# A graph network on one core: wider spread operations, row products spread over the sort, hats made earlier, a gather ring of 4 slots of 8 tiles

## The chip, the core and the metric

The kernel runs on one core of a Trainium2 chip. The metric is the device time of one execution in microseconds (us). The core has five engines with queues of their own: TensorE (PE in the profile; its weight loads PEld), VectorE (DVE), ScalarE (ACT), GpSimd (POOL) and SyncE (SP). They meet through semaphores only. Each engine works its own queue in order, so an instruction that waits holds all that is behind it.

## The reference

There are 12,500 nodes with 32 features and 200,000 edges (`src`, `dst`, and three edge attributes). Edges come sorted by `dst`. Two layers are added to `x`.

```python
def spline_conv(x, row, col, basis, idx, W, b):      # W: [125, Fin, Fout]
    z = jnp.einsum('ni,kio->nko', x, W).reshape(N * K, Fout)
    msg = jnp.einsum('es,eso->eo', basis, z[col[:, None] * K + idx])
    out = segment_sum(msg, row, N)
    return out / jnp.maximum(deg, 1.0)[:, None] + b

# layer 0: h = relu(layernorm(x)), row = src, col = dst
h1 = elu(spline_conv(ones, ..., stn1_w, stn1_b))      # 1 -> 64
h2 = elu(spline_conv(h1, ..., stn2_w, stn2_b))        # 64 -> 64
t = elu(h2 @ stn3_w + stn3_b) @ stn4_w + stn4_b       # a shift of 3 words per node
new_pseudo = clip(pseudo + t[col] - t[row], 0, 1)
x = x + spline_conv(h, ..., basis(new_pseudo), conv_w, conv_b)   # 32 -> 32

# layer 1: h = relu(layernorm(x)); graph attention with 4 heads, then a GRU gate
alpha = softmax over the edges of a dst of leaky_relu(el[src] + er[dst], 0.2)
agg = segment_sum(feat[src] * alpha, dst)
x = x + elu(gru(agg, h))
```

The basis of an edge is the product of three one-dimensional degree-1 "hats" over five knots each, so 125 numbers of which eight are not zero.

## The kernel before

All edges are padded to 1568 tiles of 128. The program is a row of phases, each a block of five engine programs with a barrier behind it.

**Sort** (`sort_edges`). Edges are put in the order of `src` by counting. A step of the loop is a group of G = 8 tiles; there are 196 groups, and two buffers `u` take turns. VectorE makes one-hot matrices of a tile's low and high key digits (`hots`, L462 and L464). TensorE transposes the low ones (L519), adds each pair of tiles to a running table in PSUM (`run`, L541), and looks the keys of each tile up in the table so far (`look`, L546). ScalarE copies the table out between two steps (L578). For the rank inside a tile, TensorE lays the tile's keys out along rows, one float32 product a tile (`rows`, L525), and VectorE compares and counts (L486). VectorE multiplies the look by the high one-hot (L491) and adds both into `place` (L496). GpSimd then scatters the eight tiles' records to memory (L600). TensorE's loop over a group has four steps `k`; each adds two tiles, looks two tiles up, and after step 1 the function `turn` issues the transposes and the row products of the next group, all together.

**First convolution** (`conv_of_ones`). 98 blocks of 128 nodes, each with 18 tiles of edges, with two buffers. SyncE loads the records of a block (L704), once TensorE has ended the block two before. ScalarE copies words into `keep` and computes parts of the hats (`hat_sides`), VectorE the rest of the hats (L744), the plane of two hats (L747), the one-hot of nodes (`mark`, L725) and the basis (L730). TensorE sums 18 products into `acc` (L782), ScalarE takes the sums (L821), and every second block TensorE mixes them with the weights. ScalarE also stores `keep` to memory (L818). In ScalarE's program a block is: hats, store, take the sums; every second block also two results.

**Second and third convolution** (`flow_conv`, called twice). GpSimd gathers node rows for all edges, a tile at a time (L913), and stores them (L920). SyncE waits until the tiles that a block needs have been stored, then loads the windows of a block: 32 windows of four nodes, 128 edges each, in two halves `q` of 16 (L974), and for the third convolution a row of shifts for each half (`trow`, L978). VectorE multiplies the mark of an edge's node by its features (`make_spread`, L1032), two windows at a time, into `spread`, eight pieces a half; in the third convolution these pieces stand between the steps of the new hats. TensorE multiplies basis and spread of each window into one of four PSUM banks (L1158); a bank holds one piece, and ScalarE empties it into `sums` (L1244). With `feats` = 64 a piece fills 512 columns of a bank, with 32 it fills 256. SyncE loads the next half when all spreads of the half before it have been made.

**Attention** (`attention_flow`). GpSimd gathers rows of `gat_table` into a ring of AT_RING = 8 slots of AT_SLOT = 4 tiles (L1528); SyncE stores each full slot (L1497) and loads the next indices for it (L1475). After a turn of 32 tiles GpSimd loads the runs of edges of two blocks of nodes (L1543), once all slots are stored and VectorE has made the products of the pair before. VectorE computes softmax weights and products (L1687), TensorE sums 41 products a block (L1774), ScalarE takes them (L1733), and VectorE and ScalarE compute the gate.

## Time and profile before

| | |
|---|---|
| three runs, median (lowest, highest) | 15029.32 us (15001.8, 15085.03) |
| the profiled execution | 14974.48 us |
| its span | 14972.8 us |
| mean granted TensorE clock | 0.721 |
| busy: TensorE, VectorE, ScalarE, GpSimd | 56%, 46%, 20%, 49% |

The profile is of one execution. A line such as L525 is a line of the kernel. "Idle before" is the time an engine was idle ahead of a group of instructions, with what ended the wait; "issue" stands for waits that ended with nothing that the profile shows, "remote" for one where the semaphore was raised well after the modelled end of all that could have raised it. The granted clock is a share of 2.4 GHz; it is 0.50 or 1.00 at any moment. A float32 product has two records.

### The profile page before, as it was taken

Reading aid. Unit: us, or ns where it says so; the run is one execution under the profiler, and the core shown is the slowest. Engines: PE = TensorE matmul, PEld = TensorE weight load, DVE = VectorE, ACT = ScalarE, POOL = GpSimd, SP = SyncE. Lnnn points to the kernel's source line nnn. Section 1 sums busy time; section 2 is a strip of 40 time slices with the busy share of each in tenths; the row PEclk is TensorE's granted clock in tenths of the full one; section 3 lists DMA queues with packets and bytes.
Section 4 is the critical chain, followed back from the end, with each engine's and each line's share of the span. In section 5 each row is a group of like instructions: output and inputs, shape, how many; then the busy total and the mean of one; then the engine's idle time right before and its main releaser. Section 6 shows DMA issues by size and latency. Waiting matters only on the chain. (4 is left out here: it accounts for less than half of the span.)

```text
span 14972.8 us, 221170 instructions
## 1 busy us (share of the span) xinstructions
PE 8457.1 (56%) x56706; PEld 7263.5 (49%) x56706; DVE 6837.4 (46%) x17239; ACT 2974.3 (20%) x9191; POOL 7273.4 (49%) x7456
## 2 busy tenths in 40 slices
PE   3466666653553777777897555555552444444445
PEld 2455555553553656665786444444552333333334
DVE  9644444443444444444676444444672222232223
ACT  0011111111111223232343222222340000000001
POOL 4355555550000888888301778878103444444442
PEclk9866666666776888888998666666885666666666
DMA  1200000006111444444332333333221111111111
GB/s 34 79 2 2 2 2 2 2 2 17 19 19 35 81 76 79 77 79 77 67 57 50 50 48 50 51 48 52 45 42 23 38 41 37 37 36 40 37 37 38
DMA packets 1831366, 603.46 MB, mean 40 GB/s; under 512 B 1616773, under 2 KB 1772389, under 8 KB 1831074
## 3 DMA queue, kind: packets, MB, share of 16 engines
q1 hardware_dynamic: 1119378, 307.87, 11.1%
q0 software_dynamic: 255648, 274.30, 10.1%
q10 hardware_dynamic: 456304, 20.89, 2.6%
q8 instruction: 13, 0.21, 0.0%
q14 instruction: 23, 0.19, 0.0%
HBM read 429.15 MB, written 172.95 MB: 40 GB/s over the span
## 5 line engine op out<-in xcount | busy, mean ns | idle before, releaser
L1158 PE MATMUL c_acc<-c_spread_sb,c_basis_sb 128*125 128x256 f32 (+1 forms) x12544 | 2750.6, 383 | 967.1 <-issue 420.5
L1158 PEld LDWEIGHTS c_acc<-c_spread_sb,c_basis_sb 128*125 128x125 f32 x12544 | 2294.3, 231 | 1335.4 <-issue 699.8
L1774 PE MATMUL at_acc_ps<-at_prod,ident 128*128 128x128 f32 x8036 | 1294.3, 312 | 1913.1 <-issue 1521.4
L600 POOL DMA_INDIRECT rec<-rk_rec,rk_place x1568 | 1620.0, 1033 | 1211.7 <-DVE rk_place L496 776.7
L1774 PEld LDWEIGHTS at_acc_ps<-at_prod,ident 128*128 128x128 f32 x8036 | 1185.7, 225 | 2022.0 <-issue 2021.6
L1528 POOL DMA_INDIRECT at_ring<-gat_table,at_place x1568 | 1486.1, 948 | 1362.2 <-issue 1311.3
L913 POOL DMA_INDIRECT c_ring<-hid_table,c_at x1568 | 1639.5, 1046 | 478.9 <-issue 463.3
L913 POOL DMA_INDIRECT c_ring<-feat_table,c_at x1568 | 1587.6, 1013 | 478.1 <-issue 463.8
L1032 DVE TENSOR_TENSOR c_spread_sb<-c_mark,c_rin 128x512 f32<-128x512 f32 (+1 forms) x3136 | 1746.0, 557 | 53.8
L1244 ACT ACTIVATE c_sums<-c_acc 125x512 f32<-125x512 f32 (+1 forms) x3136 | 1441.1, 489 | 1363.7 <-PE c_acc L1158 1062.7
L1172 PE MATMUL c_mix<-c_sums,c_w 125*64 125x128 f32 (+1 forms) x18816 | 1275.2, 300 | 525.5 <-issue 409.6
L1172 PEld LDWEIGHTS c_mix<-c_sums,c_w 125*64 125x64 f32 (+1 forms) x18816 | 992.1, 138 | 808.7 <-issue 648.9
L546 PE MATMUL rk_look_ps<-rk_table,rk_lo_t 128*128 128x98 f32 x3136 | 878.7, 412 | 713.2 <-DVE rk_before L491 682.0
L908 POOL COPY c_at<-dst_at 128x16 uint32 (+1 forms) x196 | 60.4, 308 | 2335.8 <-POOLq L1854 2335.0
L546 PEld LDWEIGHTS rk_look_ps<-rk_table,rk_lo_t 128*128 128x128 f32 x3136 | 668.5, 278 | 834.5 <-DVE rk_before L491 777.3
L491 DVE CUSTOM_DVE_ANT_0 rk_junk_l<-rk_look_ps,rk_hi 128x98 bf16<-128x98 f32 x1568 | 403.7, 257 | 1424.8 <-remote 1246.7
L782 PE MATMUL c_acc<-c_mark,c_basis_sb 128*125 128x128 f32 x3528 | 643.3, 367 | 714.5 <-DVE c_basis_sb L730 714.5
L1612 DVE COPY gr_hs<-h 128x64 f32 (+1 forms) x49 | 9.6, 195 | 2251.4 <-ACT acc L1733 2251.4
L782 PEld LDWEIGHTS c_acc<-c_mark,c_basis_sb 128*125 128x125 f32 x3528 | 627.5, 279 | 727.7 <-issue 727.7
L1543 POOL DMA_INDIRECT at_run<-rows,at_run_at x98 | 93.8, 958 | 1402.3 <-issue 1402.3
L578 ACT ACTIVATE rk_table<-rk_run_ps 128x98 f32<-128x98 f32 x784 | 198.3, 253 | 2327.1 <-remote 1204.9
L525 PE MATMUL rk_rows_ps<-ident,rk_cols 128*128 128x128 f32 x3152 | 654.6, 393 | 0.0
(358 smaller groups left out, 10906.2 us busy)
## 6 DMA issues: line engine op xcount, KB each, us to landing
c_rin<-rows SPq DMA_DIRECT2D x3136, 42.0 KB
c_rin<-rows SPq DMA_DIRECT2D x3136, 20.0 KB
rows<-c_ring POOLq DMA_DIRECT2D x392, 128.0 KB
rows<-rk_blank SPq DMA_DIRECT2D x112, 252.0 KB
rows<-c_ring POOLq DMA_DIRECT2D x392, 72.0 KB
rows<-at_ring SPq DMA_DIRECT2D x392, 72.0 KB
rec<-rk_rec,rk_place POOLq DMA_INDIRECT x1568
c_ring<-hid_table,c_at POOLq DMA_INDIRECT x1568
```

Of the source, the lines that this page charges most:

```text
L491: dve.tensor_tensor_reduce(junk_l[:, u, j, :], look[:, j % 2, 0:NB], hi_hot[:, u, j, :], 1.0, 0.0, ALU.mult, ALU.add, before[:, u, j:j + 1 ...
L525: last = pe.matmul(rows[:, u, j, :], bc(cols[:, u, j:j + 1], [P, P]), c.ident[:, :], start=True, stop=True)
L546: pe.matmul(look[:, j % 2, 0:NB], lo_t[:, u, j, :], table[:, k % 2, :], start=True, stop=True).then_inc(looked, 1)
L600: pool.indirect_dma_start(out=d.rec, out_offset=bass.IndirectOffsetOnAxis(ap=place[:, u, j:j + 1], axis=0), in_=rec[:, u, j, :], in_offset ...
L782: last = pe.matmul(acc[u][:, 0:P], basis[:, u, t, :, :].rearrange("p a b -> p (a b)"), mark[:, u, t, :], start=(t == 0), stop=(t == BT - 1))
L913: pool.indirect_dma_start(out=ring[:, u, j, :], out_offset=None, in_=table, in_offset=bass.IndirectOffsetOnAxis(ap=at[:, h, u, j:j + 1], a ...
L1032: dve.tensor_tensor(spread[:, q, w, :, :], bc(mark[:, q, w, :].unsqueeze(2), [P, 2, feats, WN]), bc(rin[:, q, w, 0:feats].unsqueeze(3), [P ...
L1158: last = pe.matmul(acc[pp % BANKS][:, (w % 2) * WN * feats:(w % 2 + 1) * WN * feats], basis[:, q, w, :, :].rearrange("p a b -> p (a b)"), ...
L1172: last = pe.matmul(mix[k * outs:(k + 1) * outs, 0:P], wsb[:, f, :], sums[:, f, :], start=(i == 0), stop=(i == each - 1))
L1244: act.activation(sums[:, :, pp * 2 * WN:(pp + 1) * 2 * WN].rearrange("p f (k n) -> p k f n", n=WN), acc[pp % BANKS][:, 0:pair].rearrange(" ...
L1528: pool.indirect_dma_start(out=ring[:, u, j, :], out_offset=None, in_=d.gat_table, in_offset=bass.IndirectOffsetOnAxis(ap=place[:, u, j:j + ...
L1774: last = pe.matmul(acc_ps[:, v, 0:P], c.ident[:, :], prod[:, v, s, :, :].rearrange("p h f -> p (h f)"), start=(s == 0), stop=(s == RUN))
```

## The change

Four parts.

1. Third convolution: a spread operation covers four windows (`span` = 4), a bank holds four windows (512 columns), a half has four pieces in place of eight, and the eviction takes 512 columns. Spread 0 follows the selection, spread 1 the subtraction of positions, spread 2 the clipping, spread 3 the plane. The second convolution keeps two windows.
2. Sort: the row products of the next group are no longer in `turn` but in `rows_of`, two of the eight after each of the four steps.
3. First convolution: ScalarE prepares (copies, hats) blocks 0 and 1 ahead of its loop. In the loop, for each block it stores, takes the sums, and prepares the block two on; then it takes the two results. `bend` has two buffers.
4. Attention: 4 slots of 8 tiles, and GpSimd no longer waits for the gathers of two slots before. A turn still has 32 tiles.

```diff
-AT_RING = 8
-AT_SLOT = 4
+AT_RING = 4
+AT_SLOT = 8
...
-                pe.wait_ge(cols_made, g + 1)
-                for j in range(G):
+            def rows_of(g, u, k):
+                if k == 0:
+                    pe.wait_ge(cols_made, g + 1)
+                for j in (2 * k, 2 * k + 1):
                     last = pe.matmul(rows[:, u, j, :], bc(cols[:, u, j:j + 1], [P, P]), c.ident[:, :],
                                      start=True, stop=True)
-                last.then_inc(rows_made, 1)
+                if k == G // 2 - 1:
+                    last.then_inc(rows_made, 1)
...
                         if k == 1:
                             turn(g + 1, 1 - u)
+                        rows_of(g + 1, 1 - u, k)
...
-            def body(b, pair, u):
+            def prepare(b, pair, u):
                 item = pair * 2 + u
                 act.wait_ge(loaded[u], pair * 16 + 16)
                 act.wait_ge(kept, item * 16 + 16)
...
+            def store(b, pair, u):
+                item = pair * 2 + u
                 act.wait_ge(copied, item * 2 + 6)
                 act.wait_ge(hats_made, item * 2 + 2)
                 act.wait_ge(kept, item * 16 + 32)
+                act.sem_inc(act_turn, 1)
...
+            with act.Fori(0, n) as o:
+                offsets.next_pass(act, o)
+                for u in range(2):
+                    prepare(u, o * (NB // 2), u)
+                with act.Fori(0, NB // 2 - 1) as h:
+                    pair = o * (NB // 2) + h
+                    for u in range(2):
+                        store(h * 2 + u, pair, u)
+                        take_sums(pair * 2 + u, u)
+                        prepare(h * 2 + u + 2, pair + 1, u)
+                    for u in range(2):
+                        take(h * 2 + u, pair * 2 + u, u)
...
-    pieces = GW2 // 2
+    span = 2 if moved is None else 4
+    pieces = GW2 // span
...
-    pair = 2 * WN * feats
+    pair = span * WN * feats
...
-                        w = slice(k * 2, k * 2 + 2)
+                        w = slice(k * span, k * span + span)
...
                 .then_inc(seq, 1)
-                make_spread(1)
                 after_step(5)
                 dve.tensor_tensor(pos[:, q, :, :], pos[:, q, :, :], tsrc[:, :, :], ALU.subtract).then_inc(seq, 1)
-                make_spread(2)
+                make_spread(1)
                 after_step(6)
...
-                make_spread(3, 4, 5)
+                make_spread(2)
...
-                make_spread(6)
                 after_step(8)
                 make_plane(hat[:, q, :, :, :])
-                make_spread(7)
+                make_spread(3)
...
-                    if u >= 2:
-                        pool.wait_ge(gathered[u - 2], t * (16 * AT_SLOT) + 16 * AT_SLOT)
-                        pool.sem_inc(pool_turn, 1)
```

## Rows read from the trace of the kernel before

**Rows 1.** Busy time by stage: sort, first convolution, third, attention.
```profile
522.00:3357.00 2835.00, 1723.37 (x9434) 1552.50 (x9434) 1320.68 (x6868) 462.50 (x1966) 1621.20 (x1570) 0.65 0.05 13
3357.00:4765.00 1408.00, 684.62 (x3921) 671.33 (x3921) 623.24 (x788) 240.81 (x980) 0.00 (x0) 0.74 0.28 19
...
8161.00:11265.00 3104.00, 1678.64 (x12916) 1387.34 (x12920) 1527.57 (x3728) 877.66 (x2938) 1920.60 (x2058) 0.69 0.32 48
...
11410.00:14973.00 3563.00, 1486.08 (x8629) 1308.81 (x8629) 1039.59 (x2426) 257.26 (x540) 1579.93 (x1666) 0.62 0.17 37
```
**Rows 2.** Waits in the sort: total us, times, longest.
```profile
DVE rk_junk_l L491 <- remote: 1246.7, 190, 8.1
...
POOL rec L600 <- DVE rk_place L496: 776.7, 196, 14.2
```
**Rows 3.** Timeline of TensorE in one group of the sort.
```profile
2025.21 1.33 PE L546 MATMUL rk_look_ps<-rk_table,rk_lo_t 128*128 128x98 f32 x4 [2.26 <-DVE rk_before L491]
...
2027.19 3.73 PE L525 MATMUL rk_rows_ps<-ident,rk_cols 128*128 128x128 f32 x16
...
2030.88 0.84 PE L546 MATMUL rk_look_ps<-rk_table,rk_lo_t 128*128 128x98 f32 x4
```
**Rows 4.** Timeline of VectorE in the same group.
```profile
2022.60 1.23 DVE L462 TENSOR_TENSOR rk_lo<-ramp_bf,src_lo 128x1024 bf16<-128x1024 bf16 x1 [0.50 <-issue]
2023.74 0.97 DVE L464 TENSOR_TENSOR rk_hi<-ramp_bf,src_hi 128x784 bf16<-128x784 bf16 x1
...
2033.59 0.26 DVE L491 CUSTOM_DVE_ANT_0 rk_junk_l<-rk_look_ps,rk_hi 128x98 bf16<-128x98 f32 x1 [6.46 <-remote]
```
**Rows 5.** The line L821 in the first convolution, and what it waited for.
```profile
L821 ACT ACTIVATE c_sums<-c_acc x98: 277/278/278, 3480.3 to 4763.1; 125x128 f32<-125x128 f32 x98
...
  PE c_acc L782: 1006.3, 97
```
**Rows 6.** Timeline of one block of the first convolution.
```profile
3903.47 0.28 ACT L821 ACTIVATE c_sums<-c_acc 125x128 f32<-125x128 f32 x1 [10.36 <-PE c_acc L782]
...
3904.40 13.51 SPq L704 DMA_DIRECT2D c_rin<-rec  x2
...
3905.71 0.41 DVE L744 SCALAR_TENSOR_TENSOR c_keep<-c_keep,c_sides 128x54 f32<-128x54 f32 x2 [6.20 <-ACT c_keep L654]
...
3909.44 7.09 PE L782 MATMUL c_acc<-c_mark,c_basis_sb 128*125 128x128 f32 x36 [6.00 <-DVE c_basis_sb L730]
```
**Rows 7.** Two microseconds of that block: busy times, then the granted clock.
```profile
3907.00:3908.00 1.00, 0.00 (x0) 0.00 (x0) 1.00 (x2) 0.00 (x0) 0.00 (x0) 1.00 0.00 0
...
3910.00:3911.00 1.00, 1.00 (x6) 1.00 (x6) 0.97 (x3) 0.00 (x0) 0.00 (x0) 0.50 0.00 0
```
**Rows 8.** Groups of the third convolution by form.
```profile
L1032 DVE TENSOR_TENSOR c_spread_sb<-c_mark,c_rin 128x256 f32<-128x256 f32 x1568 | 660.5, 421 | 13.5
```
**Rows 9.** The same operation in the second convolution.
```profile
L1032 DVE TENSOR_TENSOR c_spread_sb<-c_mark,c_rin 128x512 f32<-128x512 f32 x1568 | 1085.4, 692 | 40.3
```
**Rows 10.** Third convolution: SyncE in the gathers; SyncE and VectorE behind them.
```profile
9217.00 11.14 SPq L974 DMA_DIRECT2D c_rin<-rows  x16
...
10821.44 0.33 SPq L978 DMA_DIRECT2D c_trow<-move  x1
10822.67 8.99 SPq L974 DMA_DIRECT2D c_rin<-rows  x16
...
10824.86 0.23 DVE L1060 TENSOR_SCALAR c_rel<-c_rin,first 128x16 f32<-128x16 f32 x1 [2.65 <-DMA c_trow<-move]
```
**Rows 11.** The row loads of the third convolution, to 10560 and from there.
```profile
L978 SPq DMA_DIRECT2D c_trow<-move x133: 3/333/718, 8209.0 to 10557.2; - x133
...
L978 SPq DMA_DIRECT2D c_trow<-move x63: 332/333/333, 10569.0 to 11248.1; - x63
```
**Rows 12.** Attention: GpSimd's timeline at a run load, and waits of the stage.
```profile
12334.99 0.97 POOL L1543 DMA_INDIRECT at_run<-rows,at_run_at  x1 [29.34 <-issue]
...
PE at_acc_ps L1774 <- issue: 1521.4, 902, 3.2
```

More of the change, by code:

```diff
@@ L520, in turn @@
                 last.then_inc(turned, 1)
-                pe.wait_ge(cols_made, g + 1)
-                for j in range(G):
+            def rows_of(g, u, k):
+                if k == 0:
+                    pe.wait_ge(cols_made, g + 1)
+                for j in (2 * k, 2 * k + 1):
                     last = pe.matmul(rows[:, u, j, :], bc(cols[:, u, j:j + 1], [P, P]), c.ident[:, :],
                                      start=True, stop=True)
-                last.then_inc(rows_made, 1)
+                if k == G // 2 - 1:
+                    last.then_inc(rows_made, 1)
             pe.matmul(run[:, 0:NB], c.ident[:, :], c.base[:, 0, :], start=True, stop=True).then_inc(updated, 1)
             turn(0, 0)
+            for k in range(G // 2):
+                rows_of(0, 0, k)
             with pe.Fori(0, NG // 2) as i:
@@ L672, in conv_of_ones @@
     sides_made, bent, hats_made = sem("c1_sides"), sem("c1_bent"), sem("c1_hats")
+    act_turn = sem("c1_act_turn")
     steps = 3
@@ L678, in conv_of_ones @@
         rel = sb("c1_rel", [P, BT])
-        sides, bend = sb("c1_sides", [P, 2, BT, 3, 2]), sb("c1_bend", [P, BT, 3])
+        sides, bend = sb("c1_sides", [P, 2, BT, 3, 2]), sb("c1_bend", [P, 2, BT, 3])
         keep = sb("c1_keep", [P, 2, BT, KEEP])
@@ L819, in body, with take_sums @@
                               keep[:, u, :, :]).then_inc(kept, 16)
+            def take_sums(item, u):
                 act.wait_ge(summed, item + 3)
                 act.activation(sums[:, u, :], acc[u][:, 0:P], ACT.Copy).then_inc(sums_taken, 1)
-                if u == 1:
-                    take(b - 1, item - 1, 0)
-                    take(b, item, 1)
-            block_loop(act, c.block_passes[:, 0:1], body, before=lambda o: offsets.next_pass(act, o))
+            n = act.value_load(c.block_passes[:, 0:1], min_val=1, max_val=EP // BROWS + 1)
+            with act.Fori(0, n) as o:
[10 more added lines that the diff above has]
+                        take(h * 2 + u, pair * 2 + u, u)
+                pair = o * (NB // 2) + NB // 2 - 1
+                for u in range(2):
+                    store(NB - 2 + u, pair, u)
+                    take_sums(pair * 2 + u, u)
+                for u in range(2):
+                    take(NB - 2 + u, pair * 2 + u, u)
             act.wait_ge(indexed, 16)
@@ L1030, in make_spread @@
                     for k in ks:
-                        w = slice(k * 2, k * 2 + 2)
-                        dve.tensor_tensor(spread[:, q, w, :, :], bc(mark[:, q, w, :].unsqueeze(2), [P, 2, feats, WN]),
-                                          bc(rin[:, q, w, 0:feats].unsqueeze(3), [P, 2, feats, WN]), ALU.mult)\
+                        w = slice(k * span, k * span + span)
+                        dve.tensor_tensor(spread[:, q, w, :, :], bc(mark[:, q, w, :].unsqueeze(2), [P, span, feats, WN]),
+                                          bc(rin[:, q, w, 0:feats].unsqueeze(3), [P, span, feats, WN]), ALU.mult)\
                             .then_inc(spread_made, 1)
@@ L1244, in take_sums @@
                         act.activation(
-                            sums[:, :, pp * 2 * WN:(pp + 1) * 2 * WN].rearrange("p f (k n) -> p k f n", n=WN),
-                            acc[pp % BANKS][:, 0:pair].rearrange("p (k f n) -> p k f n", k=2, n=WN), ACT.Copy)\
+                            sums[:, :, pp * span * WN:(pp + 1) * span * WN].rearrange("p f (k n) -> p k f n", n=WN),
+                            acc[pp % BANKS][:, 0:pair].rearrange("p (k f n) -> p k f n", k=span, n=WN), ACT.Copy)\
                             .then_inc(taken, 1)
```

14 lines of the change are left out of this document (7 added, 7 removed).

## The prediction

> **What bounds the kernel now.** I read the page's 40 slices first, then the busy time by stage, then in each stage the waits and one period of the timeline. The program is five stages with barriers between them, on one core, so the gains add up. No engine is full in any stage [rows 1]: in each one a loop of waits sets the pace.
>
> The sort handles 196 groups in 2835 us, 14.46 us each [rows 1]. VectorE is busy 6.7 us of that (1320.68/196). Its largest wait, 1246.7 us in 190 waits, 6.56 us each, is for the look product of tile 4 [rows 2]. In the timeline TensorE runs the transposes and then all 16 row-product records in one block of 3.73 us before that look; VectorE, idle 6.46 us, resumes at 2033.59, though the last look record was begun by 2030.88 and lasts 0.84 us by the model [rows 3, 4]. So 1.9 us of the wait is TensorE being later than its modelled ends. GpSimd issues eight scatters and then waits 776.7/196 = 3.96 us for the places [rows 2, 4]; without that wait a group takes 14.46 - 3.96 = 10.5 us, the floor of the stage.
>
> The first convolution runs 98 blocks. After the first they come every 13.23 us ((4763.1 - 3480.3)/97), and ScalarE waits 1006.3/97 = 10.4 us of that for TensorE [rows 5]. The timeline is a ring with nothing beside it: ScalarE takes the sums at 3903.47, only then makes the hats, VectorE, idle 6.20 us for them, goes on at 3905.71, TensorE starts at 3909.44 after 6.00 us idle and works 7.09 us [rows 6]. ScalarE makes the next hats behind the sums in its own queue, though the records had long landed.
>
> The third convolution takes 3104 us [rows 1]. While GpSimd gathers (to 10560) SyncE issues 133 half-block loads, one in (10557.2 - 8209.0)/132 = 17.8 us; afterwards one in (11248.1 - 10569.0)/62 = 10.95 us [rows 11]. In the second part SyncE is full: sixteen loads are 8.99 us, the rest is offsets and the row load [rows 10]. So that tail is SyncE's, not VectorE's or ScalarE's.
>
> Attention takes 3563 us [rows 1]. GpSimd is idle 29.34 us before its run load in each period and 1402.3 us in all [rows 12]; TensorE waits 1521.4 us for nothing that the profile shows [rows 12].
>
> **The change, part by part.**
>
> *Sort.* The same 16 row records are issued, two products (4 records) after each pair of looks. No instruction and no DMA is added. From the stretch before look 4, 12 records go: 12 x 3.73/16 = 2.8 us [rows 3]. The four records of step 0 fall in TensorE's 2.26 us wait for VectorE [rows 3], those of step 3 behind the last look, under VectorE's two one-hot operations (1.23 and 0.97 us, 2.2 us [rows 4]); the four of step 2 stand before look 6, where VectorE now hardly waits: up to 0.93 us comes back. That is 1.9 us a group. The 1.9 us by which TensorE lags after the block may go too, which makes 3.8. Bounds: 1.0 us (a second of the spread pairs is paid in full) and 3.96 us (GpSimd's floor, [rows 2]). I take 2.9, midway of 1.9 and 3.8, since the lag follows the block each time: 196 x 2.9 = 568 us, range 196 to 776. If VectorE's operations no longer cover the last pair, it costs 0.93 us a group, 182 us.
>
> The lag is TensorE waiting for nothing the profile names. The Trainium skill, page "Runtime: NRT & Kernel Launch", section "Instruction fetch mechanics", says that instructions are fetched ahead and that this hides except at branches; by it the lag would not be hunger for instructions and could stay, and the sum would be 196 us poorer. The trace bears it out only in part: attention's unnamed TensorE gaps lie inside a straight run of products [rows 12].
>
> *First convolution.* ScalarE now makes the hats for block i+2 right after the sums of block i, ahead of block i+1's, so VectorE builds a basis while TensorE multiplies. Its store waits for the same hats and now stands before the sums; the final two takes of a pair stand last. Nothing is added but a second bend tile and one semaphore step. Three loops remain. VectorE: 623.24 us less the 6 us of clearing, over 98, is 6.3 us a block [rows 1]. TensorE: 7.09 us plus some 0.4 us of mixing, 7.5, at 1.2 GHz; at 2.4 GHz about half. The load ring spans two blocks: sums to load issue 0.93 us, about 3.1 us to its landing (an estimate from the third convolution, where VectorE goes on 3.1 us after the end of the row load's issue [rows 10]), hats 2.05 (the 2.24 us from 3903.47 to 3905.71, less some 0.2 for the sums' own copy), VectorE up to the first basis half 3.7, product 7.1 [rows 6]: 16.0/2 = 8.0 us; with the product at 2.4 GHz 6.2. The granted clock is 0.50 at 3910 and 1.00 at 3907, during and after the last third of a block [rows 7]: TensorE earns 2.4 GHz late in each block and loses it in the idle 6 us that now go. So I take 7.5 us, between 6.6 (VectorE with its gaps) and 8.4: 97 x (13.23 - 7.5) = 556 us, range 97 x 4.8 = 468 to 97 x 6.6 = 640. The first 120 us, to 3480.3 [rows 1, 5], stay. If a loop I do not see adds 1 us, 97 us are lost; 360 us is my lower end.
>
> The Trainium skill, page "TensorE: Matmul & The Clock Gate", Part 1, has the slow clock as the default that sustained work lifts. [rows 7] agree; by that rule alone this stage would run at 2.4 GHz throughout and VectorE would set about 6.7 us, 78 us better than the sum.
>
> *Third convolution.* VectorE's 1568 spreads of 421 ns become 784 of about 692 ns, as the second convolution's operation of 512 columns [rows 8, 9]: 660 to 543 us of busy time and half of the waits. ScalarE's evictions shrink likewise. A TensorE bank holds four windows, so it can run 16 windows ahead of ScalarE, not 8. None of this touches SyncE's tail: 63 halves stay at 10.95 us. In the gather phase a half costs 17.8 us where SyncE alone needs about 14.3 (11.14 for sixteen loads [rows 10], the rest as in the tail, with its longer gaps); 3.5 x 133 = 465 us is waiting for the others. If a quarter of it goes (my choice between none and all, nearer to none, since VectorE's spreads are two fifths of its busy time there [rows 1, 8] and half of them go), 116 us are eight more halves during the gathers, hence some 85 to 100 us off the tail. I take 100; ends 0 (the loads' own order holds) and 300 (all waiting gone). A loss would need spread 3 to hold back the basis: 0.69 us against 0.42, which is hidden under SyncE's 11 us.
>
> *Attention.* The gathers (1568), their order and the turns of 32 tiles stay. Stores go from 392 of 72 KB to 196 of 144 KB, place loads halve, and GpSimd loses six waits a turn, each of which cost under 0.3 us. The last store of a turn is twice as large and starts after eight gathers; that is covered by the 29 us of [rows 12]. SyncE issues half as many DMAs while TensorE is starved. I take 1 us of 45 periods, 40 us; ends -30 and 150.
>
> Sum: 568 + 556 + 100 + 40 = 1264 us. The profiled execution took 14974.48 us (span 14972.8), so 13,710 us; it stands 0.36% under the median 15029.32 of three runs, so in their terms 13,760.
>
> **Rivals.**
>
> *A. Forecast:* all four as above, 13,760; its own range 13,500 to 14,000. Chance 0.55.
>
> *B. The sort falls to GpSimd's floor* and the first convolution to VectorE's: 776 + 640 + 150 + 40 = 1606, so 13,420. For it: the lag comes with the block, and the average load of TensorE in the sort is only 61%. Against: ScalarE copies the records only after the scatters of two groups ago have landed, which leaves no slack at 10.5 us. Chance 0.15.
>
> *C. The spread products are not hidden:* each pair is followed by its own lag, and the sort gives 1.0 us a group, the rest as in A: 196 instead of 568, so 14,130. For it: the lag appears only while GpSimd issues scatters, and GpSimd would now issue nearly all the time. Against: 2.26 us of TensorE's wait lies in such a stretch. Chance 0.24.
>
> *D. Slower:* the last pair of row products, now behind look 7 in TensorE's queue, becomes what VectorE waits for at each group's start. It costs nothing up to 2.2 us after look 7, and one for one beyond. To cancel the other gains (696 us) a group must take 14.46 + 3.55 = 18.0 us, so the pair must come 3.55 us plus all of the saved 2.8 us late, over 8 us after look 7; with 10 us it would be 15,100. Nothing in the rows is that late but gaps under starvation. Chance 0.03.
>
> *E. The convolution's order does nothing:* ScalarE still stands behind something, say the store's landing, and its stage gains under 2 us a block: about 14,100. Chance 0.03.
>
> The range that leaves out no more than 2 in 10 reaches from B to past C: 13,350 to 14,250. A measurement here tells a change from none at about 0.5%. Faster by more 0.96, within 0.01, slower 0.03.
>
> **What would show it.** The sort: VectorE's wait for the look under 3.5 us and GpSimd's wait for places near 1 us, a stage of about 2270 us. First convolution: a block in 7.5 us, TensorE idle under 1 us, clock near 1.0 for most of it, a stage of about 850 us. Third: fewer than 63 halves after the last gather, the tail still 10.95 us each. Attention: period still near 71 us. The prediction is wrong if the sort's wait only moves to other looks, if a block takes over 9 us, or if attention's period shifts by more than 3 us, which nothing in my rows lets me foresee.

## The result and the profile after

The changed kernel takes 14,424.83 us (median of 4 runs, 14,398.6 to 14,469.58) where the kernel before takes 15,015.56 us (median of 4): ratio 0.9606, interval 0.9558 to 0.9654. That is 591 us or 3.9 per cent off, well under the 1,264 us forecast and outside the range, on its slow side.

The first view is the same table of stages, after: sort, first, second and third convolution, attention. It has busy times in the order TensorE, weight loads, VectorE, ScalarE, GpSimd, then the granted clock, the DMA share and GB/s.

```profile
522.00:3246.00 2724.00, 1753.68 (x9434) 1556.07 (x9434) 1320.55 (x6868) 464.39 (x1966) 1616.46 (x1570) 0.65 0.05 13
3246.00:4179.00 933.00, 573.56 (x3921) 553.34 (x3921) 627.49 (x788) 234.37 (x980) 0.00 (x0) 0.79 0.43 28
4230.00:7650.00 3420.00, 2702.65 (x19894) 2187.10 (x19894) 1758.67 (x2849) 1110.93 (x2744) 1963.66 (x2059) 0.87 0.35 71
7650.00:10792.00 3142.00, 1619.28 (x12920) 1342.48 (x12924) 1439.72 (x2944) 772.03 (x2154) 1892.32 (x2057) 0.67 0.29 47
10937.00:14468.00 3531.00, 1485.69 (x8629) 1304.14 (x8629) 1039.70 (x2426) 254.96 (x539) 1577.82 (x1666) 0.62 0.15 38
```

Against [rows 1]: the sort gains 111 us (568 forecast), the first convolution 475 (556), attention 32 (40). The third convolution is 38 us longer where I had 100 off, and the second, whose code is unchanged, 75 longer (3420 against 3345). Sum: 505 us, as the two profiled executions differ (14,974.48 and 14,469.58). The medians differ by 591, because the first profiled execution lay 41 us under its median and the second 45 over; so 86 us of these stage differences belong to the pair of executions and not to the change.

The sort's largest waits after the change, in the manner of [rows 2]:

```profile
ACT rk_table L584 <- PE rk_run_ps L546: 1224.3, 387, 5.3
ACT rk_table L584 <- remote: 920.3, 196, 7.6
DVE rk_junk_l L491 <- remote: 811.7, 192, 7.9
POOL rec L606 <- DVE rk_place L496: 614.6, 180, 4.5
...
DVE rk_junk_l L491 <- PE rk_look_ps L551: 492.5, 304, 2.8
```

Before, the row beside the first of [rows 2] was

```profile
DVE rk_junk_l L491 <- PE rk_look_ps L546: 119.6, 133, 6.4
```

So VectorE's two largest waits for looks have gone from 1246.7 + 119.6 = 1366 us to 811.7 + 492.5 = 1304, in more and shorter pieces, and GpSimd's wait before its first scatter from 776.7 to 670 us (614.6, and 55.7 in 16 groups for ScalarE's records), 4.0 to 3.4 us a group. One group of the timeline says where the long piece lies now: the last steps of TensorE, then ScalarE, VectorE and GpSimd, each with the idle time before it in brackets.

```profile
2009.83 1.17 PE L527 MATMUL rk_rows_ps<-ident,rk_cols 128*128 128x128 f32 x4
...
2012.79 0.37 PE L546 MATMUL rk_run_ps<-rk_hi,rk_lo 128*128 128x98 bf16 x2
2012.96 1.42 PE L551 MATMUL rk_look_ps<-rk_table,rk_lo_t 128*128 128x98 f32 x4
2014.17 1.11 PE L527 MATMUL rk_rows_ps<-ident,rk_cols 128*128 128x128 f32 x4
2017.29 0.32 PE L546 MATMUL rk_run_ps<-rk_hi,rk_lo 128*128 128x98 bf16 x2 [2.00 <-ACT rk_table L584]
```
```profile
2016.89 0.25 ACT L584 ACTIVATE rk_table<-rk_run_ps 128x98 f32<-128x98 f32 x1 [4.89 <-remote]
```
```profile
2011.89 0.26 DVE L491 CUSTOM_DVE_ANT_0 rk_junk_l<-rk_look_ps,rk_hi 128x98 bf16<-128x98 f32 x1 [2.13 <-PE rk_look_ps L551]
...
2017.62 0.26 DVE L491 CUSTOM_DVE_ANT_0 rk_junk_l<-rk_look_ps,rk_hi 128x98 bf16<-128x98 f32 x1 [3.77 <-remote]
```
```profile
2006.04 1.26 POOL L606 DMA_INDIRECT rec<-rk_rec,rk_place  x1 [3.52 <-DVE rk_place L496]
...
2015.24 0.97 POOL L606 DMA_INDIRECT rec<-rk_rec,rk_place  x1 [0.30 <-issue]
```

Read the ScalarE line against the second of TensorE's. The copy at 2016.89 waits for the run products recorded at 2012.79, 0.37 us long by the model: 4.1 us pass before ScalarE may go on, and they end 0.7 us after the eighth scatter does (2015.24 + 0.97 = 2016.21). VectorE's wait before look 4 has shrunk from 6.46 to 2.13 us as forecast, and before look 6, where I had written "VectorE now hardly waits", 3.77 us have appeared. The eighth scatter of the group before the change, which [rows 4] do not show, was

```profile
2032.64 0.97 POOL L600 DMA_INDIRECT rec<-rk_rec,rk_place  x1 [0.31 <-issue]
```

It ends at 2033.61, and VectorE's long wait had ended at 2033.59. So the wait ended with GpSimd's burst before the change as well, and the group shown is no exception: in 171 groups of the sort (between 600 and 3300 us) the wait before look 4 ended 0.0 us (median) from the end of the burst, and after the change, in 171 of 175 groups, that before look 6 ends 1.4 us behind it. The spread products let two more looks through during the burst; the last two still come when it is over.

The first convolution: ScalarE's sums, what it waits for, and its timeline over one block.

```profile
L834 ACT ACTIVATE c_sums<-c_acc x98: 277/277/278, 3369.3 to 4174.0; 125x128 f32<-125x128 f32 x98
```
```profile
ACT c_keep L816 <- DMA rows<-c_keep: 198.3, 49, 4.3
ACT c_keep L816 <- DMA c_rin<-rec: 187.6, 47, 4.7
```
```profile
3909.76 0.57 ACTq L829 DMA_DIRECT2D rows<-c_keep  x1
3910.45 0.28 ACT L834 ACTIVATE c_sums<-c_acc 125x128 f32<-125x128 f32 x1 [1.38 <-DVE c_keep L751]
3914.66 0.24 ACT L816 ACTIVATE c_keep<-c_rin 128x18 f32<-128x18 f32 x1 [3.94 <-DMA rows<-c_keep]
...
3916.33 0.39 ACT L660 ACTIVATE c_keep<-c_bend,knots 128x54 f32<-128x54 f32 x1
...
3917.94 0.57 ACTq L829 DMA_DIRECT2D rows<-c_keep  x1
```

A block takes (4174.0 - 3369.3)/97 = 8.30 us instead of 13.22. And a wait is here that [rows 6] did not have: ScalarE stores the records of a block and then, next in its order, wants to write the next but one into the same buffer, so it waits 3.94 us for its own store to land. From one store to the next it is 8.18 us. That is every second block (49 waits); in the others the load of the records lands last (47 waits), which is the load ring of the prediction.

### The profile page after: what moved, and what is told of

It is laid out like the page before. It is cut to its first block and busy times, and to the rows that moved or that the text cites. A ratio compares the mean times of both kernels' runs of the same rounds, so it can differ in the third digit from the quotient of the medians.

```text
span 14467.9 us, 214500 instructions
## 1 busy us (share of the span) xinstructions
PE 8371.9 (58%) x56706; PEld 7125.0 (49%) x56706; DVE 6752.7 (47%) x16455; ACT 2861.0 (20%) x8407; POOL 7219.1 (50%) x7456
## 3 DMA queue, kind: packets, MB, share of 16 engines
q1 hardware_dynamic: 1062354, 307.85, 10.5%
## 5 line engine op out<-in xcount | busy, mean ns | idle before, releaser
L1186 PE MATMUL c_acc<-c_spread_sb,c_basis_sb 128*125 128x256 f32 (+1 forms) x12544 | 2557.0, 368 | 464.7 <-issue 227.4
L1186 PEld LDWEIGHTS c_acc<-c_spread_sb,c_basis_sb 128*125 128x125 f32 x12544 | 2170.7, 220 | 768.6 <-issue 487.5
L606 POOL DMA_INDIRECT rec<-rk_rec,rk_place x1568 | 1615.3, 1030 | 1105.1 <-DVE rk_place L496 614.6
L1200 PE MATMUL c_mix<-c_sums,c_w 125*64 125x128 f32 (+1 forms) x18816 | 1454.3, 329 | 1136.6 <-issue 610.6
L1200 PEld LDWEIGHTS c_mix<-c_sums,c_w 125*64 125x64 f32 (+1 forms) x18816 | 1085.2, 150 | 1491.0 <-issue 914.4
L1062 DVE TENSOR_TENSOR c_spread_sb<-c_mark,c_rin 128x512 f32<-128x512 f32 x2352 | 1622.8, 690 | 40.3
L1272 ACT ACTIVATE c_sums<-c_acc 125x512 f32<-125x512 f32 x2352 | 1328.8, 596 | 1255.5 <-PE c_acc L1186 852.5
L491 DVE CUSTOM_DVE_ANT_0 rk_junk_l<-rk_look_ps,rk_hi 128x98 bf16<-128x98 f32 x1568 | 402.9, 257 | 1314.0 <-remote 811.7
L527 PE MATMUL rk_rows_ps<-ident,rk_cols 128*128 128x128 f32 x3152 | 768.8, 389 | 2.6 <-ACT rk_cols L561 2.1
L527 PEld LDWEIGHTS rk_rows_ps<-ident,rk_cols 128*128 128x128 f32 x3152 | 663.0, 291 | 5.2 <-ACT rk_cols L561 5.2
L486 DVE SCALAR_TENSOR_TENSOR rk_junk<-rk_rows_ps,src_f,rk_earlier 128x128 bf16<-128x128 f32 (+1 forms) x1568 | 647.9, 413 | 2.8 <-PE rk_rows_ps L527 2.8
L950 POOL DMA_DIRECT2D rows<-c_ring x784 | 626.9, 800 | 11.6 <-DMA c_ring<-hid_table,c_at 6.8
```

The costliest lines, as they stand in the source:

```text
L486: dve.scalar_tensor_tensor(junk[:, u, j // 2, odd:2 * odd + 1, :], rows[:, u, j - odd:j + 1, :], c.src[:, bass.ds(g * G + j, 1)], earlier[ ...
L527: last = pe.matmul(rows[:, u, j, :], bc(cols[:, u, j:j + 1], [P, P]), c.ident[:, :], start=True, stop=True)
L606: pool.indirect_dma_start(out=d.rec, out_offset=bass.IndirectOffsetOnAxis(ap=place[:, u, j:j + 1], axis=0), in_=rec[:, u, j, :], in_offset ...
L950: pool.dma_start(rows_v[:, bass.ds(t * tiles + u * slot, slot), :], ring[:, u, :, :]).then_inc(stored[u], 16)
L1062: dve.tensor_tensor(spread[:, q, w, :, :], bc(mark[:, q, w, :].unsqueeze(2), [P, span, feats, WN]), bc(rin[:, q, w, 0:feats].unsqueeze(3), ...
L1186: last = pe.matmul(acc[pp % BANKS][:, (w % span) * WN * feats:(w % span + 1) * WN * feats], basis[:, q, w, :, :].rearrange("p a b -> p (a ...
```

## The experiments

**Four parts, each alone on the kernel before.** The edits are the hunks of the diff: sort; first convolution; third convolution; attention's ring.

> The kernel before with the spread row products of the sort alone. If the parts act each in their own stage, the sort takes about 2724 us instead of 2835, every other stage is as before (second convolution near 3340, first 1408, third 3104, attention 3563) and the run stands 111 us below the kernel before. If the stage's loss against my 568 us came from another part of the change, this run gains 400 us or more. If the second convolution is near 3415 here too, its loss of 75 us comes with the sort's part.

> The kernel before with the new order of ScalarE in the first convolution alone. Parts act in their own stage: first convolution 933 us instead of 1408, the run 475 us below the kernel before. Rival, the gain is given back later: the second convolution takes 3415 us instead of 3340 and the run gains only 400 us.

> The kernel before with four windows per spread operation and per bank in the third convolution alone. Parts act in their own stage: third convolution 3142 us instead of 3104, so the run is 38 us above the kernel before (0.25 per cent). Rival, the 38 us are chance between two executions: third convolution within 3090 to 3120 and no difference in the run. My prediction's term would be 100 us off (3004).

> The kernel before with attention's ring of 4 slots of 8 alone. Parts act in their own stage: attention 3531 us instead of 3563, the run 30 us below. Rival: the ring is nothing and the 30 us are chance; the run is within 10 us of the kernel before. If the second convolution is at 3415 here, its loss hangs on nothing in this change, since this part does not touch it.

These ran on a chip on which the kernel before takes 14,374 us (25 runs; it was not profiled there). Ratios and intervals: sort 0.9976 (0.9956 to 0.9996), hats 0.9729 (0.9713 to 0.9745), third convolution 0.9960 (0.9934 to 0.9986), ring 0.9992 (0.9967 to 1.0017). In their profiles a group of the sort takes 13.81 us with the spread and 14.01 to 14.04 in the three without; a half block of the third convolution 13.62 us with four windows and 13.85 to 14.14 in the others; a block of the first 8.46 and 13.22. The second convolution, from its first gather to that of the third, is 3102 to 3193 us in all four; none has it near the 3415 us of the rivals, though the same code varies by 91 us. So the hats are some four fifths of the gain of the parts, the four windows gain and do not lose, and the sort's part gains even less than the 111 us seen first. Two of the numbers are not what was expected. The hats' run stands 411 us under the kernel before and not 475, although its blocks give 97 x (13.22 - 8.46) = 462; the profiled execution, in which the second convolution is the shortest of the four, lies 101 us under its own median, so it does not show where the rest goes. And the ring is not told from nothing by the time of the run, but from its first gather on the attention stage takes 3472 us there and 3493 to 3502 in the other three.

**Sort stages with and without scatters, in one execution.** Three copies of the stage ahead of the real one; the copies write the same records to the same places, or none (with no scatters, GpSimd only raises the semaphore).

```diff
+            phase(lambda *a: sort_edges(*a, own=True, rows_at="block", scatter=False))
+            phase(lambda *a: sort_edges(*a, own=True, rows_at="spread", scatter=False))
+            phase(lambda *a: sort_edges(*a, own=True, rows_at="block"))
             phase(sort_edges)
```

> The changed kernel with three more sort stages ahead of the real one, which write the same records to the same places or none: (1) row products in one block, no scatters, (2) row products spread, no scatters, (3) block, with scatters, (4) spread, with scatters, the real one. Only the time of a group in each stage is read. Theory 1, TensorE's lag comes while GpSimd issues scatters, wherever the row products stand: with scatters about 14.0 (block) and 13.8 us (spread), as in the runs so far; without scatters 10.5 or less for the block and 1.9 to 2.8 us less for the spread. Rival 1, the chain between ScalarE's table copies and TensorE's runs sets the pace by its own latencies: without scatters still 13 us for both. Rival 2, my own working (the block is the delay and its lag comes with it): spread saves 2.9 us with scatters and without.

This chip ran the kernel before in 11,764 us. The starts of VectorE's place operation, 196 in each stage:

```profile
L500 DVE TENSOR_TENSOR rk_place<-rk_in_tile,rk_before x196: 166/168/170, 537.9 to 2534.7; 128x8 uint32<-128x8 f32 x196
L500 DVE TENSOR_TENSOR rk_place<-rk_in_tile,rk_before x196: 166/168/169, 2550.2 to 4154.9; 128x8 uint32<-128x8 f32 x196
L500 DVE TENSOR_TENSOR rk_place<-rk_in_tile,rk_before x196: 166/168/236, 4172.3 to 6268.5; 128x8 uint32<-128x8 f32 x196
L500 DVE TENSOR_TENSOR rk_place<-rk_in_tile,rk_before x196: 166/168/239, 6297.9 to 8431.0; 128x8 uint32<-128x8 f32 x196
```

Divided by 195 intervals: 10.24 (block) and 8.23 us (spread) without scatters, 10.75 and 10.94 with them. Without scatters the spread saves 2.0 us a group, my first sum of 1.9. With them, on this chip, it saves nothing, since eight scatters at 1.27 us are 10.2 us and GpSimd is nearly full. Rival 1, ScalarE's and TensorE's own latencies, falls: 8.23 is far under 13. Rival 2, my working, falls too.

**More products, other places.** Small products are four of one column at each step, into a row bank that is overwritten later.

```diff
+                        for _ in range(small):
+                            pe.matmul(rows[:, 1 - u, G - 1, 0:1], c.ident_bf[:, :], c.ident_bf[:, 0:1],
+                                      start=True, stop=True)
```

> The changed kernel with four more sort stages ahead: (1) spread with 16 more products of one column in each group (four at each step), no scatters, (2) the same with scatters, (3) all row products in steps 0 and 1, with scatters, (4) row products two pairs at step 0, one at step 1, one at step 2, none at step 3, with scatters, (5) the real stage. Theory 1, TensorE is short of instructions while GpSimd issues: the small products add 1.5 us or more a group with scatters and under 1 us without. Rival, they cost their time on the engine alone: the same addition in both. Placement: by theory 1 each is within 0.5 us of the real stage's 13.8; by the rival that the pair at step 3 is what VectorE waits for at the end of a group, (4) is 1 us or more faster.

Same chip: 8.49 us with 16 more products and no scatters (0.26 more), and with scatters 10.72 (small), 10.73 (all in steps 0 and 1), 10.98 (none at step 3), 10.96 (real). On this chip GpSimd hides everything, so the run does not tell theory and rival apart; it shows that 16 products cost 0.26 us where nothing covers them.

**The third convolution four times in one execution.**

```diff
+            phase(lambda *a: flow_conv(*a, "c3", ..., own=True, span=2))
+            phase(lambda *a: flow_conv(*a, "c3", ..., own=True, span=4, gather=False))
+            phase(lambda *a: flow_conv(*a, "c3", ..., own=True, span=2, gather=False))
             phase(flow_conv, "c3", ...)
```

> The changed kernel with three more third convolutions ahead of the real one (they write the same rows again, or read them without gathering): (1) two windows per spread, with gathers, (2) four windows, no gathers, (3) two windows, no gathers, (4) four windows, with gathers, the real one. Theory 1, SyncE's loads set the pace where nothing is gathered and the wider operation only helps during the gathers: without gathers both take 196 x 10.95 = 2146 us and the head, with gathers (4) is 40 to 100 us shorter than (1). Rival, four windows hold up the basis or the mixing: (2) is longer than (3), and (4) is at least 38 us longer than (1), as between the first two traces.

Same chip; SyncE's row loads, 196 halves each, in the order of the diff:

```profile
L1016 SPq DMA_DIRECT2D c_trow<-move x196: 332/333/362, 6342.5 to 8799.8; - x196
L1016 SPq DMA_DIRECT2D c_trow<-move x196: 332/333/333, 8834.3 to 10973.4; - x196
L1016 SPq DMA_DIRECT2D c_trow<-move x196: 332/333/333, 11009.6 to 13147.6; - x196
L1016 SPq DMA_DIRECT2D c_trow<-move x196: 332/333/409, 13214.7 to 15582.1; - x196
```

A half takes 12.60 us with two windows and gathers, 10.97 and 10.96 without gathers (four windows, two windows), 12.14 with four and gathers. The floor of SyncE's loads, 10.95 us in [rows 11], holds whatever VectorE does, and under gathers four windows save 0.46 x 195 = 90 us.

**The changed kernel on that chip.**

> The changed kernel itself, beside the parts on one chip. If the parts add up, the ratio to the kernel before is 0.9976 x 0.9729 x 0.9960 x 0.9992 = 0.966 and its second convolution is as long as in the kernels with one part (3102 to 3193 us). Rival, the second convolution loses some 75 us in it when all parts are in: ratio 0.971.

11,285.38 us, ratio 0.9592 (0.9576 to 0.9608); 479 us off. The parts give about the same: first convolution 97 x (13.22 - 8.70) = 438 (13.22 from the other chips, the kernel before was not profiled here), third 90, sort -37 (195 x 0.19). The product of the four parts' ratios, 0.966, was expected and is missed. The first convolution is a larger share of this shorter kernel, but on the like chip below it is 0.9591 as well, and the changed kernel was not run on the chip of the parts; so that the ratios multiply is not shown. Nothing can be said here of the second convolution's 75 us, as the chip has 2602 us for it. What differs from the first profile is every stage with gathers or scatters: the sort is 564 us shorter, second and third convolution 817 and 691, attention 1147, and the blocks of the first convolution 39 us longer, which sums to the whole difference of 3181 us but for 1. A group of the sort takes 10.93 us instead of 13.82, attention's period (11,222.5 - 9038.0)/48 = 46 us instead of 69. The sort's waits say that GpSimd sets its pace here and that ScalarE waits for the records of two groups ago to land, as the prediction's Rival B had against itself:

```profile
ACT rk_rec L580 <- DMA rec<-rk_rec,rk_place: 861.6, 193, 6.5
...
POOL rec L606 <- DVE rk_place L496: 20.4, 63, 1.5
```

The waits of attention, first on the first chip, then here:

```profile
PE at_acc_ps L1799 <- issue: 1424.2, 858, 132.7
...
POOL at_run L1568 <- issue: 1394.7, 98, 55.6
```
```profile
PE at_acc_ps L1799 <- DVE at_prod L1712: 1067.6, 49, 133.7
...
POOL at_run L1568 <- issue: 85.3, 98, 29.6
```

On the first chip TensorE stops 858 times inside its products for nothing that the profile names; here that wait is not listed; TensorE waits once a period for its operand, and GpSimd goes on without its 29 us of idle time.

**The same on a chip like the first** (kernel before 14,945 us): six sort stages, the kernel before for its stages, the changed kernel, and one further edit.

> The changed kernel with five more sort stages ahead: (1) block, no scatters, (2) spread, no scatters, (3) block, with scatters, (4) all row products in steps 0 and 1, with scatters, (5) spread with 16 more one-column products a group, with scatters, (6) the real one. On a chip where the kernel before takes 11,760 us the stages without scatters took 10.24 and 8.23 us a group, and those with scatters 10.75, 10.73, 10.72 and 10.94. Theory 1, TensorE is short of instructions while GpSimd issues, more so on some chips: where the kernel before takes 14,300 to 15,000 us, (1) and (2) are again 10.2 and 8.2 (nothing is issued there), (3) and (6) are 14.0 and 13.8, and (5) adds 0.5 us or more. Rival 1, such a chip is slower as a whole (memory, clock): (1) and (2) are also 20 per cent longer. Rival 2, only the scatters' landing is slower there: then (5) adds nothing. On a chip of the first kind the run repeats those numbers.

```profile
L500 DVE TENSOR_TENSOR rk_place<-rk_in_tile,rk_before x196: 166/168/170, 537.5 to 2533.8; 128x8 uint32<-128x8 f32 x196
L500 DVE TENSOR_TENSOR rk_place<-rk_in_tile,rk_before x196: 166/168/169, 2549.3 to 4146.6; 128x8 uint32<-128x8 f32 x196
L500 DVE TENSOR_TENSOR rk_place<-rk_in_tile,rk_before x196: 166/168/169, 4164.0 to 6964.9; 128x8 uint32<-128x8 f32 x196
L500 DVE TENSOR_TENSOR rk_place<-rk_in_tile,rk_before x196: 166/168/169, 6994.6 to 9707.1; 128x8 uint32<-128x8 f32 x196
L500 DVE TENSOR_TENSOR rk_place<-rk_in_tile,rk_before x196: 166/168/170, 9737.3 to 12467.5; 128x8 uint32<-128x8 f32 x196
L500 DVE TENSOR_TENSOR rk_place<-rk_in_tile,rk_before x196: 166/168/169, 12496.3 to 15198.0; 128x8 uint32<-128x8 f32 x196
```

10.24 and 8.19 us without scatters, to a few hundredths what the other chip has. With scatters: block 14.36, steps 0 and 1 13.91, small products 14.00, spread 13.85. So the chip is not slower as a whole (rival 1 falls); it is the scatters that cost 5.7 us a group (13.85 - 8.19) where the other chip has 2.7. But 16 more products cost 0.15 us and not the 0.5 or more that a shortage of instructions would ask: that half of theory 1 falls. Rival 2, a slower landing of the scatters, foretold just that. But no wait for their landing is listed in the sixth stage, and in the sort of the first pair only 24 us before the change and none after, where the chip of 11,764 us has 861.6 us of it. And it hardly matters where the row products stand.

> The kernel before, for its stages on this chip. If the first convolution issues no gathers and so is untouched by the chip, it has 13.22 us a block again, while the sort has between 10.75 and 14.4 us a group depending on the chip, and the second and third convolutions between 2600 and 3345 us.

14,932.6 us: 14.36 us a group, 13.22 a block of the first convolution, which issues no gathers, second and third convolution 3318 and 3259 us. All of it is as expected.

> The changed kernel again, for its ratio and its stages on this chip. If the kernel before takes 11,760 us here, 0.959 again; if it takes more, 0.960 to 0.970.

14,320.76 us, ratio 0.9591 (0.9547 to 0.9636), just under the 0.960 to 0.970 expected, with an interval that reaches into it. Its second convolution is 3355 us, and in two other kernels on this chip with the same code for it 3306 and 3339; its third 3212, the same code elsewhere on the chip 3160 and 3253, the kernel before 3259. With the 91 us between the four kernels of the parts, such spreads of one code (49 to 93 us) reach the 75 and 38 us that I had to explain.

**One more edit in the first convolution**, ScalarE's order again:

```diff
-                        store(h * 2 + u, pair, u)
+                        prepare(h * 2 + u + 1, pair + u, 1 - u)
                         take_sums(pair * 2 + u, u)
-                        prepare(h * 2 + u + 2, pair + 1, u)
+                        store(h * 2 + u + 1, pair + u, 1 - u)
```

> The changed kernel with one more edit of ScalarE's order in the first convolution: it prepares block b+1, takes the sums of b, then stores block b+1, so that a store has a whole block to land before its buffer is written again. Theory: the changed kernel's 8.3 to 8.7 us a block are the loop store (0.57) - landing (4.3) - hats (2.05) - VectorE's part and the store's semaphore (1.2), 8.2 us; now VectorE (6.3) or the load ring sets 6.7 to 7.6 us, 97 blocks gain 70 to 190 us and ScalarE's wait for the landing of its store goes. Rival, the load ring is the bound already: a block stays above 8 us.

A block takes 7.70 us instead of 8.45 on the same chip. ScalarE's waits for DMAs, first of the changed kernel, then with this edit:

```profile
ACT c_keep L816 <- DMA c_rin<-rec: 199.9, 49, 5.1
ACT c_keep L816 <- DMA rows<-c_keep: 196.5, 47, 4.7
```
```profile
ACT c_keep L816 <- DMA c_rin<-rec: 163.6, 95, 2.9
```

The wait for the store's landing is gone and the load's is what is left: 73 us off the stage, just short of what I expected (7.6 us at most). The run takes 14,284.39 us (14,273.25 to 14,295.69) against 14,320.76 (14,305.51 to 14,363.65), ratio to the kernel before 0.9563 (0.9521 to 0.9604). It is the fastest version on this chip, by 0.25 per cent; the intervals of the two ratios overlap, the runs do not. Of the stage's 73 us the medians keep 36.

**What about the scatters delays TensorE.** Spread row products in all stages; in place of the scatters GpSimd does nothing, copies, issues plain stores of the same records, or SyncE issues them.

```diff
+            phase(lambda *a: sort_edges(*a, own=True, scatter=False))
+            phase(lambda *a: sort_edges(*a, own=True, scatter=False, instead="copies"))
+            phase(lambda *a: sort_edges(*a, own=True, scatter=False, instead="plain"))
+            phase(lambda *a: sort_edges(*a, own=True, scatter=False, instead="sync"))
             phase(sort_edges)
```

> The changed kernel with four more sort stages ahead (spread row products in all): (1) no scatters, nothing in their place; (2) in their place eight copies of 512 words on GpSimd; (3) eight plain stores of the same records issued by GpSimd to one scratch place; (4) the same eight stores issued by SyncE; (5) the real stage with scatters. On a chip where (5) takes about 13.8 us against 8.2 for (1): if issuing DMAs from GpSimd delays TensorE, (3) is also 11 us or more while (2) and (4) stay under 9; if it is any activity of GpSimd, (2) is above 11 too; if it is the small packets of the records on the DMA engines, (4) is as long as (3). If only indirect stores do it, (3) stays under 9. On a chip where (5) takes 10.9, GpSimd's own issue time is the bound and (3) shows only whether plain issues are shorter.

It fell on a chip without the delay (kernel before 11,748 us) and could not tell: 8.18, 8.91, 8.16, 8.24 and 10.74 us.

> The same kernel once more. On the chip of the first run (kernel before 11,748 us) its stages took 8.18 (nothing), 8.91 (copies), 8.16 (plain stores by GpSimd), 8.24 (plain stores by SyncE) and 10.74 us a group (scatters). On a chip where the kernel before takes 14,300 us or more the last is 13.8. If issuing from GpSimd delays TensorE there, plain stores by GpSimd take 11 us or more; if only the indirect form does, they stay at 8.2; if the small packets do, both kinds of plain stores are long.

Kernel before 15,127 us this time:

```profile
L501 DVE TENSOR_TENSOR rk_place<-rk_in_tile,rk_before x196: 166/167/169, 536.6 to 2136.0; 128x8 uint32<-128x8 f32 x196
L501 DVE TENSOR_TENSOR rk_place<-rk_in_tile,rk_before x196: 166/168/441, 2151.2 to 3885.0; 128x8 uint32<-128x8 f32 x196
L501 DVE TENSOR_TENSOR rk_place<-rk_in_tile,rk_before x196: 166/167/169, 3907.7 to 5529.3; 128x8 uint32<-128x8 f32 x196
L501 DVE TENSOR_TENSOR rk_place<-rk_in_tile,rk_before x196: 166/167/169, 5636.4 to 7237.0; 128x8 uint32<-128x8 f32 x196
L501 DVE TENSOR_TENSOR rk_place<-rk_in_tile,rk_before x196: 166/167/170, 7257.0 to 9964.1; 128x8 uint32<-128x8 f32 x196
```

Nothing 8.20, copies 8.89, plain stores by GpSimd 8.32, by SyncE 8.21, scatters 13.88 us. Neither a busy GpSimd, nor its issuing of plain DMAs, nor small packets from the same tile do it; of the things tried only the scatters do. In the DMA view a plain store by GpSimd and a scatter are alike, 32 packets of 130 bytes in the same queue (SyncE's store is 144 of 29). They differ in more than the indirect form: a scatter keeps GpSimd 0.97 us instead of 0.54, so eight fill 10.2 us of a group and not 4.3, and its rows go to scattered places where the plain stores go to one scratch place. Which of these it is was not tested, and the run is one execution.

Part of the 5.7 us can be TensorE's own clock in its turn. In the delayed stage the granted clock is 0.64 and TensorE is busy 8.9 us a group, in the stage with nothing 0.89 and 6.1 us. On the chip of 11,748 us the scatter stage has 0.81 and 6.8 us. The stage with nothing has 0.89 on both chips, so it is not a lower clock of the chip that begins the delay; what share of it the clock adds was not measured.

## Why the prediction was wrong

The miss against the profile terms is 14,470 - 13,710 = 760 us, by stage: sort 457, third convolution 138, first 81, second 75, attention 8.

**Sort, the step that failed.** It is the one that reads "From the stretch before look 4, 12 records go ... That is 1.9 us a group", with the lag that "may go too". I priced TensorE's products against VectorE's waits as if each step ran at its own speed. Without scatters that is right to 0.1 us (2.0 saved). With scatters it is 0.57 us in the first pair of traces ((14.39 - 13.82), [rows 2]'s kernel against the changed one), 0.51 on the like chip, 0.2 on the chip of 14,374 us, -0.2 on the chip of 11,764. On chips like the first the group is the eight scatters, 10.2 us, and then some 3.6 us in which the work held up until their end runs off. Fewer looks are left for that stretch now, two instead of four, but the first of them comes 1.4 us after the burst's end and not with it, and the 3.96 us became 3.42. I had read the 1.9 us as a lag behind the block of row products; the wait ended with the eighth scatter (2033.59 against 2033.61), which I did not lay beside it. The rows had a part of it: the lag I saw stood in the burst, and attention's unnamed gaps stood there as well ([rows 12]); I wrote down both and still let the lag shrink with the block. My Rival C, that the spread pairs are followed by their own lag, had the right kind at 14,130 us. It was still too kind by half: 1.0 us a group against 0.57. GpSimd's floor, 10.5 us in Rival B, is real, but only on the chips without the delay (10.7 to 11.0 us there). Why the held-up work waits for the scatters at all stays open.

The Trainium skill, "Runtime: NRT & Kernel Launch", section "Instruction fetch mechanics", has instruction fetch hidden except at branches, and I had concluded that the lag would not be hunger for instructions. The runs agree: 16 more products cost 0.15 us in the delayed stage and 0.26 in the free one, and from 1500 to 2500 us of the changed kernel's sort the DMA queues carry the packets of 582 scatters and none of instructions. Its consequence in my text, 196 us poorer, was the better sum.

**First convolution, the right mechanism, mis-sized.** 475 us against 556. The term of 7.5 us a block measured 8.30. "Three loops remain" was one error; a fourth is ScalarE's store, its landing and the same buffer: 0.57 + 4.3 (to 3914.66) + 2.1 (hats, to 3916.72) + 1.2 (VectorE and the semaphore, to 3917.94) = 8.2 us. I had even priced "a loop I do not see" at 97 us for 1 us, and it was 0.8. The edit that opens this loop gives 0.75 us back. The other error is in my own sum: the terms of the load ring, 0.93 + 3.1 + 2.05 + 3.7 + 7.1, are 16.9 us and not 16.0, so 8.4 us a block at 1.2 GHz and 6.7 at 2.4, and every second block does end its wait on that ring. The clock is not near 1.0 for most of the stage, as I had forecast, but 0.79 in the mean (0.83 over the blocks alone), and TensorE still idles for the basis.

**Third convolution, within its bounds but for the pair of executions.** 100 us off were forecast between 0 and 300. Within one execution four windows save 90 us on the chip of 11,764 us, the part alone saves 0.4 per cent (57 us) on that of 14,374, and 47 us lie between the two kernels on the chip of 14,945, less than the same code varies by there (93). The spread takes 687 ns (692 forecast), and without gathers a half block has SyncE's 10.97 us whatever its width, so nothing delays the basis. The eight more halves that I wanted during the gathers do not show in the first pair: 127 came there after the change, 133 before.

**Second convolution, assumed unchanged, and no run shows otherwise.** The 75 us can be chance between two executions: one code took 3306 to 3355 us on the like chip and 3102 to 3193 on that of 14,374. I also subtract stages of two single executions, 41 us under and 45 us over their medians. That the 75 us come from this is not shown, and what makes one execution longer stays open.

**Attention** gained 32 us in the first pair and 32 on the like chip (3510 against 3542 from the first gather to the end); 40 were forecast. Its price was about right; the time of the run with the ring alone (0.9992) is not told from nothing, but its attention stage is 20 to 30 us shorter than in the other three.

The direction and its chance were right. The range was too narrow at the slow end because it rested on one lag, read from one stage, shared by Rivals A, B and C: none of my cases with a chance worth the name left the sort near 14 us a group. Rival D has a sum wrong as well: by its own rule a pair 10 us behind look 7 makes about 15,300 us, 284 over the kernel before, and not 15,100.

## What to carry to other kernels

Before moving work inside a loop, ask what the loop's period follows: here it followed the length of GpSimd's burst of indirect DMAs and its aftermath, and work moved inside the burst left the next wait at its end. When a long wait has no named cause, lay the other engines' timelines beside the moment it ends, in many periods. Putting copies of a stage with one ingredient removed ahead of the real stage gives a clean comparison inside one execution, without the difference between chips or executions. And when an engine's order is changed, list for every buffer the loop from its store to its next writing, the landing included; the new order had put the two side by side.

## What the runs showed of the hardware

The same kernel takes 11,764, 14,374 and 14,945 us on three chips, each steady to 1.3 per cent. Between the changed kernel's two profiles (14,468 and 11,287 us) the whole difference lies in stages with indirect DMAs; the sort without scatters (10.24 us a group, and 8.16 to 8.23 with spread products) and the first convolution (8.30 to 8.70 us a block after the change) are nearly the same. Where it is long, a product of the sort took effect 4.1 us after its record while GpSimd issued scatters, and in attention, beside gathers, TensorE stops 858 times inside straight runs of products. Indirect stores (0.97 us of GpSimd each) do this, plain stores by GpSimd (0.54 us) do not, although both send 128 rows in 32 packets. Whether it is the indirect form, the longer issue or the scattered places, how it reaches TensorE, and why only on some chips, these runs do not show.
